# A language-model tower on one core: attention's side work dealt out anew over the heads' turns

## The chip, the core and the metric

One core of one Trainium2 chip. The metric is the device time of one execution in microseconds, the median of several; the profile is one more execution, recorded by the hardware profiler. Engines: TensorE (PE), VectorE (DVE), ScalarE (ACT), GpSimd (POOL), and SyncE (SP), which issues DMAs.

## What is computed

2048 tokens of width 256 pass through an embedding, four linear-attention blocks, a small mixture of experts, then 16-head softmax attention over sequences of 256 tokens, and a large mixture of experts with 64 experts, 8 chosen per token and 256 places per expert. The change lies in the last two, which the kernel interleaves. Cut to that:

```python
def attn(x, Wq, Wp, bp):                       # x: layernorm of h, (8, 256, 256)
    xh = x.reshape(B, N, 16, 16)
    q = jnp.einsum('bnhd,hed->bnhe', xh, Wq)
    scores = jnp.einsum('bnhe,bmhe->bhnm', q, q) / NORM
    attn = jax.nn.softmax(scores, axis=-1)
    y = jnp.einsum('bhnm,bmhe->bnhe', attn, q).reshape(B, N, D)
    return y @ Wp.T + bp
...
    logits = x_flat @ gate_weight.T            # x_flat: layernorm of the new h
    scores = jax.nn.sigmoid(logits)
    sfc = scores + e_bias[None, :]
    group_scores = jax.lax.top_k(sfc.reshape(T, NG, E // NG), 2)[0].sum(-1)
    _, gidx = jax.lax.top_k(group_scores, TG)  # 4 of 8 groups, then 8 experts of them
...
    xe = jnp.zeros((E, CAP, H)).at[sorted_e, pos].set(tok_sorted, mode='drop')
    h = silu(einsum(xe, w1)) * einsum(xe, w3)
    ye = jnp.einsum('ecf,ehf->ech', h, w2)     # weighted and summed back per token
    shared = silu(x @ shared_gate.T) * (x @ shared_up.T) @ shared_down.T
```

## The kernel before

Attention and routing are one phase, `attention_router_phase`. Each engine has its own program, written out by hand; they meet at semaphores alone, so the order within an engine is fixed when the kernel is built. The outer loop of all of them runs over SEQS = 8 sequences `i` and HEADS = 16 heads `hd`; its counter `u = 16 * i + hd` goes from 0 to 127. Here one round of it is called a turn.

In a turn TensorE issues the head's scores shifted by their row maxima (`shifted`, L2278, into `a_pB`), ScalarE takes the exponential (L2551, into the ring `a_ET`), and TensorE computes scores of a later head for the maxima (`maxima`, L2254, into `a_pA`, two banks), which VectorE reduces (`maximum`, L2585, `nmax`). `maxima_by` says how far ahead: one and a half heads per turn until `AHEAD` turns beyond one whole sequence. When a sequence's 16 maxima are there, VectorE splits them into three bf16 parts (`split`, L2594 to L2600), TensorE transposes them in the turn of `turned_at` (`maxima_transposed`, L2264), ScalarE copies them to `nT`, and SyncE moves them into row places of `right`; the first `shifted` of that sequence waits for this DMA. Four heads at a time TensorE multiplies the exponentials with the values (`values`, L2294, `a_pO`), ScalarE copies (L2502), TensorE transposes (L2304), VectorE divides (`divide`, L2607, L2611). A finished sequence is transposed (L2315), copied (L2506), projected with `wp` (`project`, L2322) and added to `h` by VectorE (`add`, L2619), with its row statistics (L2622).

Two sequences are a chunk of CH = 512 tokens (four tiles of 128); there are NC = 4, numbered 0 to 3. A chunk's routing is SPAN = 32 steps `o`, and `routing_at(step)` tells every engine which steps its turn holds: chunk 0 from turn 44 and chunk 1 from turn 76, a step per turn; chunk 2 from turn 108, two per turn; chunk 3 behind the loop. Step 0 aggregates the statistics on VectorE (`measured`, L2653, L2655, `m_veps`; for chunk 0 after some 15 constants, L2627 to L2645). POOL makes scale and shift of the rows (`rows_measured`, L2193 to L2197, here the row scale), steps 4 to 7 write the normalised rows on ScalarE (L2512), 8 to 11 transpose and copy them (L2335, L2518), 12 is the logits (L2344), 13 the sigmoid, 14 to 24 find the chosen experts on VectorE (mask `m_Mb`, L2710), 25 is their ranks on TensorE (L2354 to L2357), 27 to 29 turn ranks into slots (`m_idx`, L2731), 30 counts the taken ones on TensorE (L2362), 31 tells how many scatters a tile needs (`ksteps`, L2742).

POOL's queue, in this order: for each chunk `l` first `rows_measured(l + 1)` (for l below 2), then two scatters of each of its four tiles once the slots are there (L2202, one indirect DMA per tile and choice), then each tile's further scatters, 0 to 6, in pairs under a condition on `ksteps`. `rows_measured(3)` stands between chunk 2's first and further scatters. After chunk 2's and after chunk 3's, `scatters_over` waits until all scatters issued so far have landed. Behind it POOL adds the experts' results to the output with indirect DMAs (L1699). SyncE loads the first experts' rows (L2160) once it is told that chunks 0 to 2 have landed.

## Time and profile before

| what | us |
|---|---|
| median of 3 runs | 1204.93 |
| lowest and highest | 1203.73, 1207.11 |
| the profiled execution | 1203.64 |
| its span, first to last instruction | 1202.0 |
| attention and routing loop within it | about 821.5 to 1005.3 |
| the last expert stretch, to the end | 1067.7 to 1202.0 |

In the whole span TensorE is busy 89%, VectorE 63%, ScalarE 48%, POOL 25%; these are means over stages with quite different limits. The eight sequences start, by their first `shifted` matmul, at 821.5, 843.6, 860.2, 880.0, 903.2, 929.5, 951.9 and 975.2 us. In a row of the windows view, after the stretch, stand its length in us, the busy time with the number of records of TensorE's matmuls, its weight loads, VectorE, ScalarE and POOL, then TensorE's mean granted clock, the DMA engines' share and GB/s. An fp32 matmul stands in the trace as two records. In a row of the page's groups, behind the bar, stand busy us, mean ns of one, and idle time before them. In a timeline row the numbers are start and duration in us, then engine, line, operation, what it writes and reads, its shape, the count, and in brackets the engine's idle time before it with what ended it.

### The profile page before, as it was taken

The numbers are of one execution on the slowest core, as the hardware profiler recorded it, in microseconds if no ns is written. First come the engines' busy times: TensorE is split into PE (matmuls) and PEld (weight loads), VectorE is DVE, ScalarE is ACT, GpSimd is POOL, SyncE is SP. The second block draws the span as 40 slices with busy tenths as digits, with TensorE's granted clock in tenths as the row PEclk, the third lists the DMA queues.
The fourth block names the chain that finished last, engine by engine and source line by source line (L and its number), as shares of the span: only waits on it lengthen the run. The fifth ranks groups of instructions, "written<-read, shape, count | busy, mean of one in ns | idle before, by whom it ended". The sixth has DMA issues, their size and how long they took to land. (4 is left out here: it accounts for less than half of the span.)

```text
span 1202.0 us, 16309 instructions
## 1 busy us (share of the span) xinstructions
PE 1073.6 (89%) x4812; PEld 706.6 (59%) x4812; DVE 754.4 (63%) x1971; ACT 574.1 (48%) x970; POOL 299.9 (25%) x302
## 2 busy tenths in 40 slices
PE   5899999999999999999999999887987787898861
PEld 4556567657656756765765666663554454576741
DVE  3677766775785776677577684656769755643320
ACT  2572563563464365356446443564664663033430
POOL 6040010010011001001020101224001767366753
PEclk9999999999999999999999999897988978899995
DMA  4300120220120221021270000087633310869775
GB/s 125 129 1 1 49 75 23 84 96 1 48 75 30 80 91 49 0 75 70 70 265 1 12 7 1 4 175 146 108 55 61 123 64 27 296 142 236 123 216 99
DMA packets 58644, 100.07 MB, mean 83 GB/s; under 512 B 12504, under 2 KB 39814, under 8 KB 58315
## 3 DMA queue, kind: packets, MB, share of 16 engines
q1 hardware_dynamic: 40379, 59.22, 18.6%
q0 software_dynamic: 18192, 40.01, 12.2%
q8 instruction: 30, 0.49, 0.2%
q14 instruction: 43, 0.35, 0.1%
HBM read 58.51 MB, written 51.82 MB: 92 GB/s over the span
## 5 line engine op out<-in xcount | busy, mean ns | idle before, releaser
L561 PE MATMUL b_ring<-left 128*128 128x256 f32 x960 | 212.1, 379 | 0.0
L551 PE MATMUL b_ring<-right,left 128*128 128x512 f32 x480 | 208.4, 592 | 0.0
L561 PEld LDWEIGHTS b_ring<-left 128*128 128x128 f32 x960 | 181.6, 190 | 24.8 <-issue 1.0
L1105 POOL TENSOR_TENSOR b_rstd<-b_veps,b_mhalf 128x4 f32<-128x4 f32 x31 | 36.7, 1185 | 560.2 <-DVE b_veps L1179 560.2
L551 PE MATMUL b_ring<-XT,b_wqkv 128*128 128x512 f32 x384 | 170.1, 592 | 0.0
L551 PEld LDWEIGHTS b_ring<-right,left 128*128 128x128 f32 x480 | 91.2, 190 | 114.8 <-issue 103.0
L851 ACT ACTIVATE left<-b_ring,b_cur 128x512 f32<-128x512 f32 x128 | 88.0, 687 | 62.5 <-PE b_ring L551 44.3
L551 PEld LDWEIGHTS b_ring<-XT,b_wqkv 128*128 128x128 f32 x384 | 71.8, 190 | 77.3 <-issue 76.5
L1291 DVE RECIPROCAL b_mixing<-b_mixing 128x1024 f32<-128x1024 f32 x16 | 104.8, 6553 | 0.5
L2551 ACT ACTIVATE a_ET<-a_pB 128x512 f32<-128x512 f32 x128 | 74.1, 595 | 42.9 <-PE a_pB L2278 42.0
L2585 DVE TENSOR_REDUCE nmax<-a_pA 128x2 f32<-128x512 f32 x112 | 74.2, 688 | 32.0 <-PE a_pA L2254 30.6
L2202 POOL DMA_INDIRECT xe<-m_row,m_idx x84 | 82.5, 982 | 41.6 <-issue 26.3
L901 ACT ACTIVATE b_mixing<-b_ring,b_ncur 128x512 f32<-128x512 f32 x64 | 44.0, 688 | 101.4 <-PE b_ring L551 101.3
L848 ACT ACTIVATE b_ffo<-b_ffo 128x512 f32<-128x512 f32 x32 | 20.1, 629 | 120.1 <-DVE b_ffo L1225 120.1
L1258 DVE TENSOR_TENSOR right<-b_ffo,right 128x1024 f32<-128x1024 f32 x16 | 19.6, 1224 | 76.1 <-ACT b_ffo L848 76.1
L2278 PE MATMUL a_pB<-right,left 99*128 99x256 bf16 x256 | 54.7, 301 | 8.9 <-ACTq L2483 4.9
L561 PE MATMUL b_ring<-b_wo,right 128*128 128x256 f32 x256 | 59.7, 388 | 2.9 <-DVE right L1295 2.9
L2254 PE MATMUL a_pA<-right,left 96*128 96x256 bf16 x224 | 47.8, 301 | 14.1 <-DVE nmax L2585 13.3
L561 PEld LDWEIGHTS b_ring<-b_wo,right 128*128 128x128 f32 x256 | 49.8, 195 | 10.3 <-DVE right L1295 3.3
L1225 DVE TENSOR_TENSOR b_ffo<-b_ring,b_rows 128x512 f32<-128x512 f32 x32 | 22.1, 690 | 51.7 <-PE b_ring L561 32.3
L1185 DVE SCALAR_TENSOR_TENSOR right<-right,b_mv,b_rows 128x256 f32<-128x256 f32 x128 | 53.3, 477 | 0.0
L1214 DVE BATCH_NORM_STATS2 b_stats<-right 128x6 f32<-128x256 f32 x128 | 45.0, 413 | 1.3
(410 smaller groups left out, 1773.2 us busy)
## 6 DMA issues: line engine op xcount, KB each, us to landing
xe<-b_nil POOLq DMA_DIRECT2D x16, 1284.0 KB, 6.0
left<-in_w SPq DMA_DIRECT2D x8, 1024.0 KB, 5.4
a_ET<-xe SPq DMA_DIRECT2D x18, 321.0 KB, 4.0
parts<-in_wexp SPq DMA_DIRECT2D x12, 384.0 KB, 4.3
b_wqkv<-in_wqkv SPq DMA_DIRECT2D x4, 768.0 KB, 4.6
b_rows<-in_rows SPq DMA_DIRECT2D x8, 384.0 KB, 5.5
right<-qparts SPq DMA_DIRECT2D x16, 192.0 KB, 4.9
left<-qparts SPq DMA_DIRECT2D x16, 192.0 KB, 5.3
```

Of the source, the lines that this page charges most:

```text
L551: last = pe.matmul(bank[:, :], lhsT(k), rhs(k), start=(k == 0), stop=(k == n_k - 1))
L561: last = pe.matmul(bank[:, j * D:(j + 1) * D], src[:, k, tile], weights[:, k, :], start=(k == 0), stop=(k == n_k - 1))
L851: act.activation(H[:, f, :], bank[:, :], ACT.Gelu_apprx_tanh, bias=col("b1", f)).then_inc(s_h, 1)
L901: act.activation(nqk[:, j, m, :], bank[:, :], ACT.Relu, scale=-1.0, bias=ncur[:, KD * j + m:KD * j + m + 1])
L1185: last = dve.scalar_tensor_tensor(src[:, j, :], src[:, j, :], mv[:, j, 0:1], gain, ALU.subtract, ALU.mult)
L1214: last = dve.bn_stats(stats[:, j, :], src[:, j, :])
L1291: chain.link(dve.reciprocal(rec, den))
L2202: pool.indirect_dma_start(g["xe"][0:SLOTS, :], bass.IndirectOffsetOnAxis(ap=idx[:, t, k:k + 1].bitcast(U32), axis=0), row[:, t, :], None, ...
L2254: last = pe.matmul(pA[hd % 2][:, nt, :], left[0:ROWS, slot, hd, nt * P:(nt + 1) * P], right[0:ROWS, slot, hd, :], start=True, stop=True)
L2278: last = pe.matmul(pB[hd % 2][:, mt, :], left[0:ROWS + SPLIT, slot, hd, mt * P:(mt + 1) * P], right[0:ROWS + SPLIT, slot, hd, :], start=Tr ...
L2551: act.activation(ET[:, hd % ERING, :, :], pB[hd % 2][:, :, :], ACT.Exp, scale=4.0).then_inc(s_e, 1)
L2585: dve.tensor_reduce(nmax[:, :, hd], pA[hd % 2][:, :, :], AX.X, ALU.max, negate=True).then_inc(s_m, 1)
```

## The change

- `AHEAD` is 16, not 8: the maxima run up to 32 heads ahead, at one and a half per turn up to turn 31. `turned_at` lets the transposition of the maxima follow two turns after they are ready, or in the third turn of the sequence before.
- SPAN is 35. The routing steps are grouped otherwise (three of VectorE's larger ones cut in two), and a table TURNS holds the turn of each step of each chunk. Ranks are step 27, slots step 32, the count of the taken 33, `ksteps` 34.
- VectorE's constants are made one or two a turn from turn 32 on, and the waits for them stand at step 14.
- `values` and `project` are issued in two halves in neighbouring turns; `add` moves by a turn, and the row statistics (`summed`) follow a turn later.
- On POOL, `rows_measured(3)` stands ahead of the last tile's further scatters of chunk 1.
- Waits of the transpositions are fitted to the new order. Behind the loop, steps 14 to 27 and 28 to 34 stand where 14 to 26 and 27 to 31 stood.

```diff
@@ -1495,9 +1495,19 @@
 LATE = 2 * (NEXP - EARLY)
 GROUPS = -(-(EARLY + LATE) // RINGX)
 
-SPAN = 32
+SPAN = 35
 ROUTED = NC - 1
 LISTED = SEQS * HEADS - 4
+
+
+TURNS = (
+    (47, 47, 47, 47, 49, 49, 50, 50, 51, 52, 53, 54, 55, 56, 57, 57, 58, 58,
...
+)
...
         ident, h, qn, xT, ones_b, before = (g[n] for n in ("ident", "h", "qn", "XT", "ones_b", "before"))
         NTS = SEQ // P
-        AHEAD, QRING = 8, 2
+        AHEAD, QRING = 16, 2
...
@@ -2090,21 +2100,13 @@
         def turned_at(n):
 
             ready = next(u for u in range(SEQS * HEADS) if maxima_by(u) >= HEADS * (n + 1))
-            return max(HEADS * (n - 1) + 3 * QUAD, ready + 2)
+            return max(HEADS * (n - 1) + 2, ready + 2)
 
         turns = {turned_at(n): n for n in range(1, SEQS)}
 
         def routing_at(step):
 
-            found = []
-            for l in range(ROUTED):
-                begun = HEADS * (2 * l + 2) + 12
-                pace = 1 if l + 1 < ROUTED else 2
-                for part in range(pace):
-                    o = pace * (step - begun) + part
-                    if 0 <= o < SPAN:
-                        found.append((l, o))
-            return found
+            return [(l, o) for l in range(ROUTED) for o in range(SPAN) if TURNS[l][o] == step]
 
...
@@ -2230,8 +2232,8 @@
                 for j in range(TPC):
                     scattered(l * TPC + j, True)
                 for j in range(TPC):
-                    if l + 1 == ROUTED and j == 0:
-                        rows_measured(l + 1)
+                    if l + 2 == ROUTED and j == TPC - 1:
+                        rows_measured(l + 2)
                     scattered(l * TPC + j, False)
                 if l + 1 >= ROUTED:
                     scatters_over(l + 1 - ROUTED)
                 pe.wait_ge(s_nr, 3 * n)
                 if n > 1:
                     pe.wait_ge(s_nte, n - 1)
-                    pe.wait_ge(s_h, n - 1)
+                if n > 2:
+                    pe.wait_ge(s_h, n - 2)
                 for nt in range(NTS):
                     last = pe.transpose(pM[:, nt * P:(nt + 1) * P], npart[:, nt, :], g["ident_b"][:, :])
                 last.then_inc(s_nt, 1)
...
-            def values(i, k):
+            def values(i, k, mt):
 
                 n, slot = QUADS * i + k, i % QRING
-                if k == 0:
-                    pe.wait_ge(s_qs, i + 1)
-                    if i < QRING:
-                        pe.wait_ge(s_q1, 2 * (i + 1))
-                pe.wait_ge(s_ot, n + 2)
-                pe.wait_ge(s_e, QUAD * (n + 1) + 2)
-                for mt in range(NTS):
-                    for part in range(QUAD):
-                        hd = k * QUAD + part
-                        last = pe.matmul(pO[part * HW:(part + 1) * HW, k % 2, :], qs[:, slot, mt, hd, :],
-                                         ET[:, hd % ERING, mt, :], start=(mt == 0), stop=(mt == NTS - 1))
-                last.then_inc(s_o, 1)
+                if mt == 0:
+                    if k == 0:
+                        pe.wait_ge(s_qs, i + 1)
+                        if i < QRING:
+                            pe.wait_ge(s_q1, 2 * (i + 1))
+                    pe.wait_ge(s_ot, n + 2)
+                    pe.wait_ge(s_e, QUAD * (n + 1) + 2)
+                for part in range(QUAD):
+                    hd = k * QUAD + part
+                    last = pe.matmul(pO[part * HW:(part + 1) * HW, k % 2, :], qs[:, slot, mt, hd, :],
+                                     ET[:, hd % ERING, mt, :], start=(mt == 0), stop=(mt == NTS - 1))
+                if mt == NTS - 1:
+                    last.then_inc(s_o, 1)
...
-                if i + 1 < SEQS:
-                    pe.wait_ge(s_nte, i + 1)
+                pe.wait_ge(s_nte, min(i + 2, SEQS - 1))
...
-            def project(i):
-                pe.wait_ge(s_yte, i + 1)
-                for nt in range(NTS):
-                    for k in range(KD):
-                        last = pe.matmul(pH[:, nt, :], yT[:, k, nt * P:(nt + 1) * P], wp[:, k, :], start=(k == 0), stop=(k == KD - 1))
-                last.then_inc(s_p, 1)
+            def project(i, nt):
+                if nt == 0:
+                    pe.wait_ge(s_yte, i + 1)
+                for k in range(KD):
+                    last = pe.matmul(pH[:, nt, :], yT[:, k, nt * P:(nt + 1) * P], wp[:, k, :], start=(k == 0), stop=(k == KD - 1))
+                if nt == NTS - 1:
+                    last.then_inc(s_p, 1)
...
-                if o == 25:
+                if o == 27:
                     ranks(l)
-                if o == 30:
+                if o == 33:
                     taken_counted(l)
...
-                    if hd in (7, 11, 15):
-                        values(i, hd // QUAD - 1)
-                    if i and hd == 3:
-                        values(i - 1, QUADS - 1)
+                    if hd >= 6 and hd % QUAD >= 2:
+                        values(i, hd // QUAD - 1, hd % 2)
+                    if i and hd in (2, 3):
+                        values(i - 1, QUADS - 1, hd % 2)
                     if hd in (9, 13):
                         quad_transposed(i, hd // QUAD - 2)
                     if i and hd in (1, 5):
                         quad_transposed(i - 1, hd // QUAD + 2)
                     if i and hd == 8:
                         y_transposed(i - 1)
-                    if i and hd == 10:
-                        project(i - 1)
+                    if i and hd in (10, 11):
+                        project(i - 1, hd % 2)
...
+            def summed(i):
                 dve.wait_ge(s_h, i + 1)
                 for t in range(NTS * i, NTS * (i + 1)):
                     last = dve.bn_stats(g["stats"][:, t, :], h[:, t, :])
                 last.then_inc(s_st, 1)
...
+            def constants(o):
+                if o == 0:
+                    dve.wait_ge(s_c, 9)
+                    dve.tensor_copy(first[:, :], first_i[:, :]).then_inc(s_cc, 1)
+                if o == 1:
+                    dve.tensor_copy(row[:, :, D], tok_i[:, :]).then_inc(s_cc, 1)
+                if o == 2:
...
+                if o == 16:
+                    dve.wait_ge(s_cc, 14)
+                    dve.tensor_scalar(expert[:, 1, :], expert[:, 1, :], float(-SPE * NEXP), None, ALU.add).then_inc(s_cc, 1)
...
-                    if l == 0:
-                        constants()
                     measured(l)
                 if o == 14:
                     dve.wait_ge(s_sc, l + 1)
+                    if l == 0:
+                        dve.wait_ge(s_cc, 15)
+                        dve.wait_ge(s_gw, 32)
                     link(dve.tensor_tensor(sfc[:, :, :], score[:, :, :], ebias[:, :].unsqueeze(1).to_broadcast([P, TPC, NEXP]), ALU.add))
...
                     link(dve.tensor_tensor(sums[:, :, 0:2], quarters[:, :, 0:2], quarters[:, :, 6:8], ALU.add))
+                    link(dve.tensor_reduce(gs[:, :, :].rearrange("p t g -> p (t g)"), sums[:, :, :], AX.X, ALU.max))
                 if o == 19:
-                    link(dve.tensor_reduce(gs[:, :, :].rearrange("p t g -> p (t g)"), sums[:, :, :], AX.X, ALU.max))
-
                     other = gs[:, :, :].unsqueeze(2).to_broadcast([P, TPC, NG, NG])
                     own = gs[:, :, :].unsqueeze(3).to_broadcast([P, TPC, NG, NG])
                     dve.tensor_tensor(gt[:, :, :].rearrange(sq4, g=NG), other, own, ALU.is_gt)
...
-                if o == 27:
+                if o == 29:
                     dve.wait_ge(s_rk, l + 1)
                     dve.tensor_tensor(slot[:, :, :], ranked, first[:, :].unsqueeze(1).to_broadcast([P, TPC, NEXP]), ALU.add)
                     link(dve.scalar_tensor_tensor(valid[:, :, :], ranked, float(CAP), M[:, :, :], ALU.is_lt, ALU.mult))
...
-                if o == 29:
+                if o == 31:
                     dve.memset(g["carrier"][:, :], 0.0)
                     for j in range(TPC):
                         last = dve.max(s8[:, j, :], slot1[:, j, :])
                     link(last)
+                if o == 32:
                     dve.tensor_scalar(idx[:, l * TPC:(l + 1) * TPC, :], s8[:, :, :], -1.0, None, ALU.add).then_inc(s_ix, 1)
                     dve.tensor_scalar(v8b[:, :], s8[:, :, :].rearrange("p t k -> p (t k)"), 0.5, None, ALU.is_gt).then_inc(s_v8, 1)
...
-                    if i and hd == 11:
+                    if i and hd == 12:
                         add(i - 1)
+                    if i and hd == 13:
+                        summed(i - 1)
+                    constants(u - 2 * HEADS)
                     for l, o in routing_at(u):
                         routed(l, o)
```

Where the instructions stand now. TensorE, sequence 1's first turns: `a_pB` is a turn's shifted scores, `a_pA` the maxima's scores, two matmuls a head. Before:

```order
L2278 MATMUL a_pB<-right,left 128x256 x2
L2254 MATMUL a_pA<-right,left 128x256 x2
L2278 MATMUL a_pB<-right,left 128x256 x2
L2254 MATMUL a_pA<-right,left 128x256 x2
L2304 MATMUL a_pR<-ident,a_OT 128x128 x2
L2278 MATMUL a_pB<-right,left 128x256 x2
L2254 MATMUL a_pA<-right,left 128x256 x2
L2278 MATMUL a_pB<-right,left 128x256 x2
L2254 MATMUL a_pA<-right,left 128x256 x2
L2294 MATMUL a_pO<-a_ET,a_qs 32x256 x8
```

and now:

```order
L2281 MATMUL a_pB<-right,left 128x256 x2
L2256 MATMUL a_pA<-right,left 128x256 x4
L2281 MATMUL a_pB<-right,left 128x256 x2
L2256 MATMUL a_pA<-right,left 128x256 x2
L2308 MATMUL a_pR<-ident,a_OT 128x128 x2
L2281 MATMUL a_pB<-right,left 128x256 x2
L2256 MATMUL a_pA<-right,left 128x256 x4
L2297 MATMUL a_pO<-a_ET,a_qs 32x256 x4
L2281 MATMUL a_pB<-right,left 128x256 x2
L2256 MATMUL a_pA<-right,left 128x256 x2
L2297 MATMUL a_pO<-a_ET,a_qs 32x256 x4
```

Every second turn has the scores of two heads, and the values come in two groups of four.

VectorE, from chunk 0's maxima over slots (`m_s`) to the start of its step counts (`m_kcnt`). Before (turns 73 to 75):

```order
L2729 MAX m_s<-m_kept 128x8 x4
L2731 TENSOR_SCALAR m_idx<-m_s 128x32
L2732 TENSOR_SCALAR m_v8b<-m_s 128x32
L2585 TENSOR_REDUCE nmax<-a_pA 128x2
L2734 TENSOR_TENSOR m_cum<-m_cum,m_mch 128x64
L2735 CAST taken<-m_cum 128x128
L2585 TENSOR_REDUCE nmax<-a_pA 128x2
L2619 TENSOR_TENSOR h<-h,a_pC 128x512
L2622 BN_STATS stats<-h 128x6 x2
L2738 TENSOR_SCALAR m_some<-m_pG 1x32
L2739 TENSOR_REDUCE m_kcnt<-m_some 1x4
L2740 TENSOR_SCALAR m_kcnt<-m_kcnt 1x4
```

and now (end of turn 79 to turn 82):

```order
L2671 BN_AGGR m_mv<-stats 128x2 x4
L2673 TENSOR_SCALAR m_veps<-m_mv 128x4
L2591 TENSOR_REDUCE nmax<-a_pA 128x2
L2747 MEMSET carrier 128x1
L2749 MAX m_s<-m_kept 128x8 x4
L2591 TENSOR_REDUCE nmax<-a_pA 128x2
L2752 TENSOR_SCALAR m_idx<-m_s 128x32
L2753 TENSOR_SCALAR m_v8b<-m_s 128x32
L2755 TENSOR_TENSOR m_cum<-m_cum,m_mch 128x64
L2756 CAST taken<-m_cum 128x128
L2591 TENSOR_REDUCE nmax<-a_pA 128x2
L2759 TENSOR_SCALAR m_some<-m_pG 1x32
```

The slots now follow chunk 1's statistics (`m_veps`); before they preceded them.

POOL, from chunk 1's last tile to chunk 2's first scatters (each pair of scatters stands under a condition). Before:

```order
L2215 COMPARE_AND_BRANCH
L2202 DMA xe<-m_row,m_idx 16384x321 x2
L2215 UNCONDITIONAL_BRANCH
L2202 DMA xe<-m_row,m_idx 16384x321 x8
L2193 TENSOR_TENSOR m_rstd<-m_veps,m_mhalf 128x4
L2195 TENSOR_TENSOR m_shift<-m_mv,m_rstd 128x4
L2197 TENSOR_SCALAR m_shift<-m_shift 128x4
```

and now:

```order
L2204 DMA xe<-m_row,m_idx 16384x321 x2
L2217 UNCONDITIONAL_BRANCH
L2195 TENSOR_TENSOR m_rstd<-m_veps,m_mhalf 128x4
L2197 TENSOR_TENSOR m_shift<-m_mv,m_rstd 128x4
L2199 TENSOR_SCALAR m_shift<-m_shift 128x4
L2215 TENSOR_LOAD ksteps
L2215 ISA x2
L2217 COMPARE_AND_BRANCH
L2204 DMA xe<-m_row,m_idx 16384x321 x2
L2217 UNCONDITIONAL_BRANCH
L2217 COMPARE_AND_BRANCH
...
L2204 DMA xe<-m_row,m_idx 16384x321 x2
L2217 UNCONDITIONAL_BRANCH
L2204 DMA xe<-m_row,m_idx 16384x321 x8
```

The row scale (`m_rstd`, `m_shift`) has moved ahead of the tile's scatters and of the eight.

## Rows read from the trace of the kernel before

**Rows 1.** Windows: sequences 1 to 6, chunk 2's chain, the stretch behind attention.
```profile
843.64:860.21 16.57, 16.02 (x150) 9.69 (x151) 13.04 (x27) 11.24 (x24) 0.00 (x0) 1.00 0.46 78
860.21:880.04 19.83, 17.05 (x150) 9.89 (x151) 15.54 (x49) 11.17 (x24) 1.46 (x3) 0.91 0.64 114
880.04:903.22 23.18, 20.22 (x179) 13.72 (x175) 14.73 (x34) 17.18 (x33) 0.00 (x0) 0.93 0.26 46
903.22:929.49 26.27, 19.21 (x170) 10.65 (x166) 24.75 (x84) 11.90 (x24) 1.97 (x4) 0.90 0.33 58
929.49:951.88 22.39, 19.51 (x178) 13.11 (x175) 14.69 (x34) 16.99 (x33) 17.21 (x18) 0.96 0.35 126
951.88:972.59 20.71, 15.22 (x135) 8.92 (x131) 19.63 (x73) 10.23 (x22) 11.80 (x13) 0.92 0.16 57
972.59:1005.30 32.71, 24.43 (x177) 14.98 (x176) 16.91 (x74) 18.06 (x34) 24.76 (x27) 0.74 0.19 64
1005.30:1067.67 62.37, 52.75 (x216) 34.81 (x217) 32.52 (x119) 13.41 (x25) 31.18 (x34) 0.92 0.55 179
```

**Rows 2.** Waits, 821 to 1006 us: waiter, releaser, total us, times, longest.
```profile
PEld a_pA L2254 <- DVE nmax L2585: 26.0, 44, 2.8
...
PE m_pG L2354 <- DVE m_Mb L2710: 6.0, 3, 2.8
...
PE a_pB L2278 <- DMA right<-nT: 3.2, 3, 2.1
```

**Rows 3.** VectorE, a run of maxima (timeline); the matmuls for the maxima (page).
```profile
844.29 2.49 DVE L2585 TENSOR_REDUCE nmax<-a_pA 128x2 f32<-128x512 f32 x4 [2.37 <-PE a_pA L2254]
...
L2254 PE MATMUL a_pA<-right,left 96*128 96x256 bf16 x224 | 47.8, 301 | 14.1 <-DVE nmax L2585 13.3
```

**Rows 4.** Windows: the constants, a split, two comparisons, slots with counts, step counts.
```profile
874.36:876.40 2.04, 0.61 (x4) 0.31 (x4) 1.90 (x16) 1.23 (x3) 0.00 (x0) 1.00 0.04 12
917.63:918.39 0.76, 0.74 (x6) 0.53 (x6) 0.66 (x4) 0.76 (x2) 0.00 (x0) 1.00 0.00 0
1027.75:1028.54 0.79, 0.79 (x6) 0.69 (x5) 0.76 (x2) 0.00 (x0) 0.00 (x0) 1.00 1.02 386
1040.25:1041.57 1.32, 1.32 (x6) 1.02 (x5) 1.22 (x9) 0.00 (x0) 0.00 (x0) 0.54 0.98 377
1044.69:1045.64 0.95, 0.95 (x3) 0.38 (x3) 0.84 (x5) 0.00 (x0) 0.70 (x1) 1.00 1.02 387
```

**Rows 5.** Timeline, POOL: scatters of the four chunks, row scales, the first expert sum.
```profile
928.99 1.13 POOL L2202 DMA_INDIRECT xe<-m_row,m_idx  x1 [0.61 <-issue]
...
966.37 0.97 POOL L2202 DMA_INDIRECT xe<-m_row,m_idx  x1 [0.30 <-issue]
972.85 1.04 POOL L2193 TENSOR_TENSOR m_rstd<-m_veps,m_mhalf 128x4 f32<-128x4 f32 x1 [5.51 <-DVE m_veps L2655]
...
1016.88 1.08 POOL L2202 DMA_INDIRECT xe<-m_row,m_idx  x1 [1.11 <-issue]
...
1041.87 0.97 POOL L2202 DMA_INDIRECT xe<-m_row,m_idx  x1 [14.96 <-DVE m_idx L2731]
...
1067.67 1.58 POOL L1699 DMA_INDIRECT sums<-a_qs,x_home  x1 [5.68 <-ACT a_qs L1799]
```

**Rows 6.** Timeline, VectorE: chunk 0's slots and chunk 2's statistics.
```profile
921.49 0.18 DVE L2731 TENSOR_SCALAR m_idx<-m_s 128x32 int32<-128x32 f32 x1
...
972.59 0.17 DVE L2655 TENSOR_SCALAR m_veps<-m_mv 128x4 f32<-128x4 f32 x1
```

**Rows 7.** Timeline, SyncE's queue; then DMA issues: KB and us to landing.
```profile
1042.34 4.52 SPq L2160 DMA_DIRECT2D a_ET<-xe  x3
...
sums<-a_qs,x_home POOLq DMA_INDIRECT x2, 4.3
```

**Rows 8.** Timeline, TensorE: the logits of chunk 0 and of chunk 2.
```profile
891.61 1.97 PE L2344 MATMUL m_pG<-m_gate,XT 128*128 128x64 f32 x16
...
980.39 3.67 PE L2344 MATMUL m_pG<-m_gate,XT 128*128 128x64 f32 x16 [0.26 <-ACT XT L2518]
```

81 lines of the change are left out of this document (43 added, 38 removed), and 5 rows, old and new, of the table TURNS.

## The prediction

> **What bounds the kernel now.** I read the busy time by stretches first [rows 1]. The change touches 843 us to 1005 us, the attention over eight sequences of 16 heads; I call the step in which TensorE issues one head's shifted scores a turn (0 to 127), and a stretch of [rows 1] is 16 turns, up to the last two. Sequence 1 takes 16.57 us with TensorE busy 16.02: TensorE sets it. Sequence 4 takes 26.27 us with VectorE busy 24.75 (0.94): VectorE sets it, because it has the maxima of 16 heads and most of a chunk's routing. Sequence 6 has VectorE busy 19.63 of 20.71. In sequences 3 and 5 nobody is full; TensorE waits in turns for VectorE and ScalarE. The waits of TensorE say the same [rows 2]: weight loads waited 26.0 us for a maximum (two PSUM banks, so TensorE is at most two heads ahead of VectorE), matmuls 6.0 us for the routing mask and 3.2 us for the row of shifts. From 972.59 to 1005.30 one chain sets the time: chunk 2's statistics, POOL's row scale, ScalarE's rows, the logits, then some 30 small VectorE operations. Behind attention, TensorE is busy 52.75 of 62.37 us, and this stretch's order is nearly unchanged. So the end moves by what the last chain's start moves, if POOL, which scatters rows, keeps up [rows 5].
>
> **Part 1: maxima 16 heads ahead.** Turns 16 to 31 now carry 24 maxima, not 16, and turns 96 to 103 carry none. One costs VectorE 0.60 us (four in 2.49 us, where the last one's end still overlaps the next, [rows 3]); TensorE pays at most 0.43 (47.8 us busy for 224 matmuls, two a head, and back to back they overlap). Sequence 1's VectorE sum becomes 13.04 + 8 x 0.60 + 0.8 (one more split of maxima into parts, [rows 4]) = 18.6 us, beside TensorE's 16.02 and at most 3.4 more. At sequence 4's ratio of 0.94 it takes 19.8 us: **+3.2** (bounds +2, if both overlap fully, and +5). In exchange the shift rows (turn 18, 34, ... instead of 28, 44, ...) have landed at each later sequence's start; only sequence 1's first wait, 2.1 of the 3.2 us [rows 2], stays. In sequence 6 VectorE loses nine maxima and a split, 6.2 us: 19.63 - 6.2 = 13.4, and I add 3 us in which VectorE and TensorE wait for each other (mask, ranks, projection): 16.4 against 20.71, **-4.3** (bounds -2 and -6).
>
> **Part 2: constants one by one.** Before, VectorE makes all constants in turn 44, 2.04 us from 874.36 on, just after a sum and before the statistics [rows 4]. They hold up maxima, TensorE waits, and its clock is at half afterwards (0.91 and 0.93 granted in sequences 2 and 3, [rows 1]). Now each turn has one of 0.1 to 0.3 us. Sequence 2's VectorE sum stays 15.54 us; over 0.94 that is 16.5, and I take 16.8 against 19.83: **-3.0** (bounds -1.5 and -3.5).
>
> **Part 3: the chunk steps.** Chunk 0's 35 steps run over turns 47 to 82 (before 32 over 44 to 75). In sequence 3 nothing is left in turns 60 to 63, and the start is at full clock: I take **-2.4** of 23.18 (bounds 0 and -3.5; TensorE is busy 20.22 of it, part of that at half clock). In sequence 4, the two group comparisons come in (0.79 us), and the last maxima over slots, the sums of counts and the step counts go out into turns 80 to 82: in chunk 3's rows these are 1.32 and 0.95 us [rows 4]. Net -1.5: 24.75 becomes 23.3, over 0.94 24.8: **-1.4** (bounds 0 and -2.5). Sequence 5 gets these 2.3 us, but had VectorE busy 14.69 of 22.39, and its last four turns lose steps too: 0 (bounds -1 and +2). Values and projection cut in halves cost TensorE nothing, since the matmuls are the same; a block of 1.1 us becomes two. I give them nothing of their own.
>
> Up to turn 80 that makes +3.2 - 3.0 - 2.4 - 1.4 = **-3.6 us**, up to chunk 2's statistics -7.9.
>
> **Part 4: what POOL then does.** This is the step that I expect to decide. Chunk 0's slots are now ready in turn 81, not in turn 73 (921.49 us, [rows 6]). Before, chunk 1's row scale stood ahead of its scatters in POOL's queue, and they began at 928.99 [rows 5]. Now: turn 80 at 929.49 - 3.6 = 925.9, plus two maxima (1.2), the maxima over slots (0.64) and the slots (0.17): 927.9, first scatter at 928.3. The 30 scatters last 38.35 us (928.99 to 966.37, + 0.97), and behind them in POOL's queue stands chunk 2's row scale: 966.7, while VectorE has its input ready at 972.76 - 7.9 = 964.9 [rows 6]. Before it was the other way round: POOL had idled 5.51 us when it began at 972.85. So of 7.9 us, 972.85 - 966.7 = 6.1 arrive. The chain behind it has the same operations; ScalarE's rows now have one more head's exponential between them: +0.6. I take **-5.5 us** for the end of attention.
>
> **Part 5: chunk 3's row scale ahead of chunk 1's last tile.** POOL now stops there until attention is over, and then has that tile's later scatters (2 to 6) and chunk 2's 16 still to issue, 18 to 22 times 1.28 us = 23 to 28 us. On the old time base: from 1016.9 to 1040 - 1045, where chunk 3's slots are ready at 1041. Before, POOL idled 14.96 us there [rows 5]; that idle time is the cover, and it is used up. What is late next is POOL's wait for the landing of these scatters, which it needs before chunk 3's. No row shows a landing of this line; the nearest is POOL's indirect sum at 4.3 us [rows 7], and zero is the other end. So chunk 3's scatters start 0 to 8 us late, and the first expert sum at 1067.67 can absorb up to 5.7 us between the last scatter's end and it [rows 5]: cost 0 to 2.5, I take 0, as the tile with the fewest kept rows should have 2. SP loads the first experts' rows at 1042.34 [rows 7], 25 us ahead of the first sum; 8 us late they still land 12 us ahead of it, and cost nothing.
> For the landing, the Trainium skill (DMA: Bandwidth & Descriptors, Anatomy of one DMA — SWDGE (gpsimd) path) has a fit of 2.0 us and the bytes over 436 GB/s; an estimate by it for 164 KB is 2.4 us, and the cost would be 0 to 1. No run here shows it.
>
> **Sum.** The profiled execution took 1203.64 us (span 1202.0 and 1.6 around it), 1.3 below the median of 1204.93. 1203.6 - 5.5 = 1198.1; on the median **1199.4 us**.
>
> **The rivals.**
> A. *Side work decides, not POOL* (0.12): the first scatter is early enough, or the later sequences gain more. Then most of 7.9 and more arrives: 1195 to 1196. For it: sequences 3 and 5 have slack on every engine. Against: 38.35 us of scatters is a hard length.
> B. *The gain shrinks* (0.22): sequence 1 costs 5, or sequence 3 gives nothing, so turn 80 moves by only 1 us; then the first scatter is at 930.9 and the row scale at 969.3, gain 3; or Part 5 costs 2.5. 1201 to 1203.5.
> C. *It does not do what it says* (0.08): VectorE's sum over turns 16 to 127 is unchanged, and if TensorE's waits only move, from sequence 6 into 1, the time is 1204 to 1206. Against: sequence 1 has 3.5 us of idle VectorE, sequence 7's chain has no maxima to move.
> D. *Slower through the scatters* (0.10): chunk 0's scatters begin eight turns later. From a first scatter at 934.5 on, POOL reaches the row scale after 972.85 and everything is late by the rest. That needs turn 80 at 932.2, 2.7 us later than before, so sequence 1 at +5, sequences 3 and 4 at 0, and sequence 5's added steps in full: 1206, and up to 1211 where the chain behind is longer too.
> E. *Slower through TensorE's clock* (0.06). The logits took 1.97 us at the high level (2.4 GHz) and 3.67 us in sequence 7, where the granted clock of the stretch was 0.74 after TensorE had waited for rows [rows 8, 1]. Without maxima in turns 96 to 103 and with more waiting for POOL, TensorE is less busy there; if sequence 6's projection, values and transposes also ran at 1.2 GHz it would cost 2 to 4 us, and the gain is 2: 1203, or with B 1206.
> The Trainium skill (TensorE: Matmul & The Clock Gate, Part 1: The HAM clock gate) says that the throttled state is the default and that activity releases it. By it E is the likelier, the more work leaves TensorE; the sum above has the clock as before.
>
> **How the numbers follow.** Forecast, 1197 to 1201.3: 0.42. A 0.12, B 0.22, C 0.08, D 0.10, E 0.06. About 0.3%, 3.6 us, is what a measurement can tell from no change, so faster is below 1201.3: forecast and A in full, a quarter of B: 0.60. Slower is above 1208.5: D's upper half and E with it, 0.09. The rest, 0.31, is within. The range takes A in and goes up to D's lower part: 1194.5 to 1206.5.
>
> **What would show it.** In the changed profile: sequence 1 near 19.8 us with VectorE above 0.9; no TensorE wait for shift rows but the first; sequence 2 near 17; POOL's first scatter near 928, chunk 2's row scale right behind chunk 0's last scatter without idle, near 967; POOL idle some 12 us before chunk 3's row scale near 1008.5, and little before chunk 3's scatters; the first expert sum near 1062. I am wrong if sequence 1 takes over 22 us, if POOL idles before chunk 2's row scale (then A), if the first scatter is after 931 (B, D), or if the stretch from row scale to attention's end is over 34 us (E).

## The result: slower by 0.9%

The changed kernel took 1214.40 us as the median of four executions (1212.46 to 1216.67), the kernel before 1204.66 in the same comparison; the ratio is 1.009, with a 95% interval of 1.0062 to 1.0117. In a second comparison, called f1_again below, it was 1.0105 (1.0073 to 1.0137). The prediction was 1199.4 with a range up to 1206.5: wrong in sign, and out of range.

The profiled execution took 1212.46 us, its span is 1210.8, and its mean granted clock is 0.954, as before. Windows of the changed kernel, with the columns of [rows 1]: sequences 1 to 6 (6 up to chunk 2's statistics), chunk 2's chain, the stretch behind attention.

```profile
845.28:868.59 23.31, 20.34 (x167) 11.38 (x167) 17.47 (x34) 11.89 (x23) 0.00 (x0) 0.93 0.35 62
868.59:885.70 17.11, 16.36 (x155) 9.41 (x151) 14.09 (x40) 11.75 (x24) 0.00 (x0) 1.00 0.54 96
885.70:912.93 27.23, 21.24 (x179) 12.87 (x175) 16.16 (x45) 17.52 (x33) 1.46 (x3) 0.94 0.35 60
912.93:935.15 22.22, 19.17 (x168) 9.82 (x165) 21.02 (x61) 12.26 (x24) 0.00 (x0) 0.92 0.42 73
935.15:963.34 28.19, 22.07 (x179) 13.18 (x176) 17.97 (x58) 17.82 (x33) 18.72 (x21) 0.88 0.28 98
963.34:984.28 20.94, 15.80 (x129) 7.96 (x125) 15.00 (x67) 11.35 (x23) 12.41 (x13) 0.84 0.29 98
984.28:1016.80 32.52, 21.69 (x172) 11.21 (x170) 16.89 (x74) 17.89 (x32) 21.39 (x23) 0.84 0.11 35
1016.80:1080.41 63.61, 54.36 (x226) 36.65 (x227) 33.23 (x123) 13.77 (x26) 34.87 (x37) 0.92 0.56 183
```

Against [rows 1], sequence 1 is 6.7 us longer, 3 by 4.1 and 5 by 5.8; sequence 2 is 2.7 shorter and 4 by 4.1. Sequence 6 up to chunk 2's statistics and the chain behind it are as long as before, to 0.2 us. From sequence 0's first shifted scores to the end of the add of sequence 7 it is 11.7 us more: 8.0 of them in sequences 1 to 6, 3.0 from sequence 7's start on and 0.7 in sequence 0. The waits of the same stretch, 822 to 1017 us, in the columns of [rows 2]:

```profile
PEld a_pA L2256 <- DVE nmax L2591: 19.1, 37, 1.4
...
PE m_pG L2358 <- DVE m_Mb L2729: 5.5, 2, 2.8
...
PE a_pC L2325 <- ACT a_yT L2512: 4.9, 2, 2.4
...
PE a_pB L2281 <- ACT a_ET L2557: 3.9, 3, 1.9
...
PE m_pG L2366 <- DVE m_v8b L2753: 3.6, 2, 2.8
...
PE a_pB L2281 <- DMA right<-nT: 1.5, 1, 1.5
```

The two waits that the change was read for are shorter: weight loads for a maximum 26.0 to 19.1, shift rows 3.2 in three to 1.5 in one. Three others have come or grown: the projection's for ScalarE's copy of y, twice 2.4 us (before 0.7 at most), the shifted scores' for an exponential, all in sequence 7, and the count's of the taken for the slots. POOL's timeline, the rows that answer to [rows 5]:

```profile
940.90 1.13 POOL L2204 DMA_INDIRECT xe<-m_row,m_idx  x1 [1.13 <-DVE m_idx L2752]
...
984.45 1.04 POOL L2195 TENSOR_TENSOR m_rstd<-m_veps,m_mhalf 128x4 f32<-128x4 f32 x1 [5.04 <-DVE m_veps L2673]
...
1026.77 1.04 POOL L2195 TENSOR_TENSOR m_rstd<-m_veps,m_mhalf 128x4 f32<-128x4 f32 x1 [14.46 <-DVE m_veps L2673]
...
1057.20 0.97 POOL L2204 DMA_INDIRECT xe<-m_row,m_idx  x1 [4.65 <-DMA xe<-m_row,m_idx]
...
1080.41 1.58 POOL L1709 DMA_INDIRECT sums<-a_qs,x_home  x1 [3.08 <-DMA xe<-m_row,m_idx]
```

POOL idles 5.04 us ahead of chunk 2's row scale, as it did before. The scatters, which I expected to decide, decide nothing here.

### The profile page after: what moved, and what is told of

Same layout as the page of the kernel before. It is cut to its first block and busy times, and to the rows that moved or that the text cites. A ratio compares the mean times of both kernels' runs of the same rounds, so it can differ in the third digit from the quotient of the medians.

```text
span 1210.8 us, 16301 instructions
## 1 busy us (share of the span) xinstructions
PE 1080.4 (89%) x4812; PEld 702.2 (58%) x4812; DVE 752.9 (62%) x1971; ACT 577.8 (48%) x970; POOL 301.0 (25%) x302
## 3 DMA queue, kind: packets, MB, share of 16 engines
q1 hardware_dynamic: 40379, 59.22, 18.6%
## 5 line engine op out<-in xcount | busy, mean ns | idle before, releaser
L561 PEld LDWEIGHTS b_ring<-left 128*128 128x128 f32 x960 | 181.8, 190 | 24.6 <-issue 1.0
L848 ACT ACTIVATE b_ffo<-b_ffo 128x512 f32<-128x512 f32 x32 | 20.1, 629 | 120.1 <-DVE b_ffo L1225 120.1
L1225 DVE TENSOR_TENSOR b_ffo<-b_ring,b_rows 128x512 f32<-128x512 f32 x32 | 22.1, 691 | 51.6 <-PE b_ring L561 32.2
L2297 PE MATMUL a_pO<-a_ET,a_qs 128*32 128x256 f32 x512 | 46.6, 442 | 0.5 <-ACT a_OT L2508 0.5
```

Of the source, the lines that this page charges most:

```text
L561: last = pe.matmul(bank[:, j * D:(j + 1) * D], src[:, k, tile], weights[:, k, :], start=(k == 0), stop=(k == n_k - 1))
L2297: last = pe.matmul(pO[part * HW:(part + 1) * HW, k % 2, :], qs[:, slot, mt, hd, :], ET[:, hd % ERING, mt, :], start=(mt == 0), stop=(mt == ...
```

## Where sequences 3 and 5 went, read from the trace

ScalarE's timeline of turns 56 to 58 in the changed kernel:

```profile
899.98 0.60 ACT L2557 ACTIVATE a_ET<-a_pB 128x512 f32<-128x512 f32 x1 [1.74 <-PE a_pB L2281]
900.59 1.28 ACT L2528 ACT_TABLE_LOAD   x1
901.89 0.38 ACT L2528 ACTIVATE m_score<-m_pG 128x256 f32<-128x256 f32 x1
902.29 1.28 ACT L2557 ACT_TABLE_LOAD   x1
903.58 0.60 ACT L2557 ACTIVATE a_ET<-a_pB 128x512 f32<-128x512 f32 x1
904.08 0.59 ACT L2512 ACTIVATE a_yT<-a_pC 128x512 f32<-128x512 f32 x1
```

and of TensorE at that time:

```profile
900.00 0.60 PE L2318 MATMUL a_pC<-ident,a_y 128*128 128x128 f32 x4
...
901.63 0.64 PE L2297 MATMUL a_pO<-a_ET,a_qs 128*32 128x256 f32 x8
904.72 0.77 PE L2325 MATMUL a_pC<-wp,a_yT 128*128 128x256 f32 x1 [2.45 <-ACT a_yT L2512]
```

The same turns of the kernel before, on ScalarE:

```profile
893.84 0.60 ACT L2551 ACTIVATE a_ET<-a_pB 128x512 f32<-128x512 f32 x1 [1.88 <-PE a_pB L2278]
894.33 0.59 ACT L2506 ACTIVATE a_yT<-a_pC 128x512 f32<-128x512 f32 x1
894.94 1.28 ACT L2522 ACT_TABLE_LOAD   x1
896.24 0.38 ACT L2522 ACTIVATE m_score<-m_pG 128x256 f32<-128x256 f32 x1
896.64 1.28 ACT L2551 ACT_TABLE_LOAD   x1
```

The sigmoid needs a table of its own and the exponential behind it the old one: 1.28 + 0.38 + 1.28 us, 3.0 with the gaps. Before, step 13 stood in turn 57 behind the copy of y. Now it is in turn 56, ahead of it, and the projection of turn 58 waits for all of it. Chunk 1 has the same in turn 90. The Trainium skill (ScalarE: Activation LUTs, What ACT_TABLE_LOAD costs) gives 1283 ns for the load, as here, and 1380 ns for a drain beside it. The trace shows no such drain: 1.31 us lie between the exponential's end and the sigmoid.

VectorE in turns 80 and 81 of the changed kernel:

```profile
937.89 0.17 DVE L2673 TENSOR_SCALAR m_veps<-m_mv 128x4 f32<-128x4 f32 x1
937.97 0.68 DVE L2591 TENSOR_REDUCE nmax<-a_pA 128x2 f32<-128x512 f32 x1
...
938.71 0.46 DVE L2749 MAX8 m_s<-m_kept 128x8 f32<-128x64 f32 x3
939.21 0.69 DVE L2591 TENSOR_REDUCE nmax<-a_pA 128x2 f32<-128x512 f32 x1
939.82 0.17 DVE L2752 TENSOR_SCALAR m_idx<-m_s 128x32 int32<-128x32 f32 x1
939.90 0.18 DVE L2753 TENSOR_SCALAR m_v8b<-m_s 128x32 bf16<-128x32 f32 x1
```

Steps 32 and 33 of chunk 0 share turn 81. TensorE issues the count (33) in that turn and waits 2.79 us for the slots (32), since VectorE is behind by chunk 1's statistics, the maxima over slots and two maxima of scores. Its clock is at half from 938.91 to 945.74, and turn 82 has 2.17 us.

## The experiments

The experiments ask four things in turn: what each part of the change costs by itself, what comes back when a part is taken out of the changed kernel, what the halved blocks do, and whether the good parts alone make a faster kernel.

A word on the measuring. The kernel before was executed 132 times beside the experiments, 1196.12 to 1213.39 us. These times go with the mean granted clock: 0.63 us less for each 0.001 more (correlation -0.76; 0.959 in the fastest, 0.947 in the slowest). One trace is one such draw: the attention's first scores began anywhere from 818.6 to 827.8 us, in front of everything that was changed, and the last expert stretch, behind it, took 130.4 to 134.8 us. So totals are told by the ratios over many executions, and a trace only tells where something happened. The table gives, from one trace each, the time from one sequence's first shifted scores to the next one's, and from sequence 0's first to the end of the add of sequence 7.

| kernel | parts | ratio, 95% interval | seq 1 | 2 | 3 | 4 | 5 | 6 | 0 to add 7 |
|---|---|---|---|---|---|---|---|---|---|
| before | | 1 | 16.6 | 19.8 | 23.2 | 26.3 | 22.4 | 23.3 | 191.1 |
| changed | all | 1.0090, 1.0062-1.0117 | 23.3 | 17.1 | 27.2 | 22.2 | 28.2 | 21.6 | 202.8 |
| f1_again | all | 1.0105, 1.0073-1.0137 | 23.6 | 17.1 | 27.2 | 22.2 | 31.1 | 20.7 | 205.9 |
| e1_ahead | A | 1.0012, 0.9983-1.0042 | 22.2 | 20.4 | 23.4 | 26.6 | 22.7 | 19.4 | 194.6 |
| e2_constants | C | 0.9965, 0.9940-0.9989 | 16.6 | 17.1 | 22.2 | 26.1 | 22.2 | 24.4 | 190.5 |
| e3_halves | H | 1.0017, 0.9988-1.0046 | 17.2 | 19.1 | 22.8 | 26.2 | 21.6 | 24.6 | 192.4 |
| e4_turns | T | 1.0025, 0.9997-1.0053 | 16.6 | 16.6 | 26.1 | 23.0 | 25.2 | 28.5 | 193.4 |
| f2_no_ahead | C H S T P | 1.0093, 1.0060-1.0126 | 18.2 | 18.6 | 28.6 | 22.7 | 25.8 | 27.3 | 202.7 |
| f3_score_back | A C H S T' P | 1.0033, 1.0009-1.0056 | 22.1 | 17.1 | 25.2 | 21.9 | 25.7 | 21.5 | 195.9 |
| f4_late_ahead | C, A late | 0.9956, 0.9935-0.9978 | 16.6 | 17.1 | 22.2 | 25.4 | 25.7 | 19.8 | 189.0 |
| g1_const_turns | C T' | 0.9985, 0.9968-1.0003 | 17.9 | 16.8 | 22.7 | 22.2 | 23.1 | 28.8 | 189.9 |
| g2_spread_late | C T'', A late | 0.9965, 0.9938-0.9993 | 16.6 | 16.8 | 21.7 | 22.2 | 29.2 | 18.9 | 184.4 |
| g3_pool_as_before | A C H S T' | 1.0042, 1.0024-1.0061 | 23.6 | 17.1 | 24.0 | 22.2 | 24.6 | 21.4 | 194.5 |
| g4_no_ahead_13 | C H S T' P | 1.0055, 1.0023-1.0087 | 18.2 | 18.5 | 22.7 | 22.8 | 23.8 | 27.2 | 195.7 |
| h1_whole_values | A C T' | 0.9988, 0.9963-1.0013 | 23.4 | 17.2 | 24.8 | 22.0 | 24.1 | 20.6 | 194.6 |
| h2_halves_kept | A C H T' | 1.0083, 1.0046-1.0119 | 23.5 | 17.5 | 23.7 | 23.4 | 24.7 | 18.5 | 199.0 |
| h3_combined | C T''', A late | 0.9946, 0.9918-0.9974 | 16.6 | 16.8 | 21.7 | 23.3 | 26.2 | 21.4 | 189.2 |
| i1_changed_whole | A C S T P | 1.0042, 1.0029-1.0055 | 23.0 | 17.2 | 25.7 | 21.8 | 29.5 | 20.1 | 194.6 |
| i2_values_halved | A C T', values halved | 1.0021, 0.9992-1.0050 | 23.6 | 17.5 | 23.6 | 22.2 | 25.5 | 20.9 | 192.6 |
| i3_project_halved | A C T', project halved | 1.0042, 1.0023-1.0061 | 24.0 | 17.8 | 24.2 | 23.2 | 24.9 | 18.5 | 199.4 |

A is the maxima ahead with their transposition, C the constants dealt out, H values and projection in halves, S add in a sequence's turn 12 and statistics in 13, T the regrouped steps with TURNS, P POOL's order. T', T'' and T''' are tables mended as told below.

### Each part alone

Each is the kernel before with hunks of the change. A, which also has the two waits of the transpositions fitted:

```diff
-        AHEAD, QRING = 8, 2
+        AHEAD, QRING = 16, 2
-            return max(HEADS * (n - 1) + 3 * QUAD, ready + 2)
+            return max(HEADS * (n - 1) + 2, ready + 2)
```

> The kernel before with part 1 of the change alone: AHEAD 16, turned_at two turns after the maxima are ready or in turn 2 of the sequence before, and the two waits of the transpositions fitted to it. Theory L (each part cost what its own sequence shows): sequence 1 grows by about 6 us over before's 16.57, to 22 to 23; no wait for shift rows after the first; sequence 6 falls by 2 to 4 from 23.32; sequence 4 falls from 26.27 a little; end of attention +1 to +4 against 1005.3. Theory I (sequence 1 grew in the changed kernel because the extra maxima meet the values in halves): with whole values sequence 1 is 18.5 to 20.5, as I had forecast (19.8), and the end of attention comes 0 to 3 us earlier.

Sequence 1 took 22.19 us, with whole values: the first theory. Only the first wait for shift rows is left, and sequence 6 fell by 3.9. Its window in this kernel, and in f3_score_back, where the clock is at full in it:

```profile
850.08:872.27 22.19, 19.36 (x166) 11.69 (x166) 17.83 (x35) 11.68 (x23) 0.00 (x0) 0.92 0.32 55
```
```profile
841.42:863.47 22.05, 18.94 (x166) 10.66 (x167) 17.31 (x34) 11.90 (x23) 0.00 (x0) 1.00 0.42 72
```

With VectorE busy 17.3 and TensorE 18.9 of 22.05, neither is full, and the clock is not the reason. VectorE's idle time has not shrunk: 16.57 - 13.04 = 3.5 us before [rows 1], 22.05 - 17.31 = 4.7 now. Most of it lies where TensorE runs values and the projection (beside the projection gaps of 1.8 us before, and of 1.3 and 1.4 us in f3_score_back). Two banks of scores are all that VectorE has to work on meanwhile; that this is why more maxima don't fill it is my reading of the order, and no run with more banks was made. They come on top: 4.3 us of VectorE's work made 5.5 us of time.

The constants alone (C; `constants(u - 2 * HEADS)` in each turn, the waits at step 14):

> The kernel before with VectorE's constants alone dealt out over turns 32 to 48, and their waits at step 14. Both theories: sequence 2 falls from 19.83 to about 17, as in the changed kernel (17.11), everything else as before, the end of attention 2 to 3 us earlier, total about 1202. Rival: the block of constants was harmless, sequence 2 fell in the changed kernel because its maxima had run ahead; then sequence 2 stays at 19 to 20 and the total is unchanged.

Sequence 2 fell to 17.14 us, and the ratio's interval (0.9940 to 0.9989) lies below 1: this part is a small gain of its own. In the one trace the 3.8 us that it led at sequence 5 shrank to 0.5 by the add of sequence 7.

H alone, with the add in turn 11 as before:

```diff
+                    if hd >= 6 and hd % QUAD >= 2:
+                        values(i, hd // QUAD - 1, hd % 2)
...
+                    if i and hd in (10, 11):
+                        project(i - 1, hd % 2)
```

> The kernel before with values and project in two halves in neighbouring turns alone (add and row statistics where they were). Theory H (two small blocks cost TensorE more than one, since each half starts anew and waits for the exponentials one turn earlier): every sequence from 1 on grows by 0.5 to 1.0 us, end of attention +3.5 to +7. Theory N (they cost nothing of their own, as I had forecast): every sequence within 0.3, end within 1 us, unless they fill a turn in which TensorE waits anyway.

Neither theory: sequences 1 and 6 are longer, 2 and 5 shorter, and the ratio's interval holds 1.

T alone (TURNS and SPAN = 35; the constants in one block, now in turn 47):

> The kernel before with the routing steps regrouped to 35 and the table TURNS alone (constants still in one block, now in turn 47). Theory S (the sigmoid, now one turn ahead of ScalarE's y copy, makes the projection wait; slots and counts of chunk 0 now in one turn behind chunk 1's statistics): waits of TensorE of about 2.4 us each in turns 58 and 90 for ScalarE's y copy and 2 to 3 us in turn 81 for VectorE; sequences 3 and 5 come to about 26 to 28 us (before 23.18 and 22.39), the first scatter near 940, the end of attention +5 to +9. Theory L (packing cost only together with the other parts): sequences 3 and 5 within 1.5 of before, end within 2.

Waits of TensorE from sequence 0 to 1000 us:

```profile
PE a_pC L2324 <- ACT a_yT L2508: 6.8, 3, 3.0
...
PE m_pG L2364 <- DVE m_v8b L2736: 3.5, 2, 2.4
```

The projection waited 3.0 us in turns 58 and 90; turn 81's wait was 1.1, and 2.4 came in turn 104, where chunk 1's slots and count are neighbours. Sequences 3 and 5 grew by 3.0 and 2.8 (26.1 us as expected, and 25.2, a little under it) and 6 by 5.2, but 2 and 4 shrank by 3.2 and 3.3, and 2.1 us went behind sequence 7's start, so the sum was +2.3 and not +5 to +9.

The four ratios add up to +0.2%, not +0.9%. S and P are in none of them. Either the changed kernel's executions were late by chance, or parts hurt each other, or S or P costs by itself.

> The changed kernel once more, beside the others of this comparison. The four single parts gave 1.0012, 0.9965, 1.0017 and 1.0025 of before, which add up to +0.2%, while the changed kernel had 1.009 in four executions. Theory of adding up by the trace: from sequence 0's first shifted scores to the add of sequence 7 the parts alone gave +3.5, -0.5, +1.3 and +2.3 us, and 2.7 of the constants' gain is in two of them, so +9.3 of the 11.7 us that the changed kernel took longer there: the ratio comes out again at 1.006 to 1.010, sequence 1 at 22 to 24, sequences 3 and 5 at 26 to 28. Rival, the first executions were late by chance: ratio 1.001 to 1.004.

It was 1.0105: not chance. P is taken out below (1.0042 against 1.0033, no difference); S was never run alone, so what is left is that parts hurt each other or that S does.

### Taking parts away from the changed kernel

Without A:

> The changed kernel without part 1: AHEAD 8, turned_at and the two waits as before. Adding up: sequence 1 at 17 to 17.5, sequence 6 at 24 to 26 in place of 21.6, sequence 0's start to sequence 7's add at 198 to 200 us (changed kernel 202.8, before 191.1), ratio 1.004 to 1.006. Rival, the maxima ahead hurt the packed steps: sequences 3 and 5 fall back below 24.5 as well and the ratio is 1.001 or less.

A miss: 1.0093, no better than with it. Sequence 1 fell to 18.2 us, but a wait had come:

```profile
PE a_pC L2266 <- DVE h L2625: 8.2, 6, 1.5
```

The old place of the maxima's transposition is turn 12, and it waits for the previous sequence's add, which S has moved to turn 12. The undoing had made a new wait, so it doesn't price A. With the transposition in turn 13, `max(HEADS * (n - 1) + 3 * QUAD + 1, ready + 2)`, and the table T':

> As the kernel with the sigmoid and the counts moved, and without the maxima ahead; unlike the first undoing, the transposition of the maxima stands in the sequence's turn 13, behind VectorE's add (turn 12), for which it waited 8.2 us in all. Adding up: sequence 1 at 17 to 18 in place of 22.05, sequence 6 two to four us above 21.5, waits of that transposition under 2 us in all, ratio 0.999 to 1.002. Rival, removing the lead costs as much in the later sequences as it gives in sequence 1: ratio 1.003 to 1.005.

1.0055 beside 1.0033 with A: outside the theory's range, a little above the rival's, and the two intervals overlap. Six such waits are left with 5.7 us, and shift rows are waited for seven times, 7.0 us. Sequence 1 gives 3.9 us back and sequence 6 takes 5.8. Where S is in, taking A out gains nothing.

The sigmoid behind the copy of y, and the counts apart from the slots (T'):

```diff
-    ... 54, 55, 56, 57, 57, 58, 58, 59, 64, ..., 76, 80, 81, 81, 82),
+    ... 54, 55, 57, 58, 58, 59, 59, 60, 64, ..., 76, 80, 81, 82, 83),
-    ... 86, 87, 88, 89, 89, 90, 91, 91, 96, ...
+    ... 86, 87, 89, 90, 90, 91, 91, 92, 96, ...
```

> The changed kernel with the sigmoid one turn later (57 and 89, behind ScalarE's y copy, with steps 14 to 18 a turn later), and chunk 0's counts in turns 82 and 83 in place of 81 and 82. Theory S: the projection's waits of 2.4 us in turns 58 and 90 fall to about 0.3, turn 81's wait of 2.8 us to under 0.8; sequences 3 and 5 lose 2 to 3 and 3 to 5 us, sequence 0's start to sequence 7's add comes to 195 to 198 us, ratio 1.002 to 1.005. Rival, these waits lie beside others and come back elsewhere in the same sequence: both sequences within 1 us of 27.2 and 28.2.

Median 1208.97 against 1216.67 in the same comparison, 7.7 us less, and intervals that don't meet. The projection's waits of 2.4 us are gone. Turns 58 and 59, as windows of the changed kernel and of this one:

```profile
901.10:909.38 8.28, 5.83 (x35) 3.16 (x33) 4.11 (x13) 5.00 (x8) 0.00 (x0) 0.79 0.01 2
897.13:901.63 4.50, 4.30 (x34) 2.35 (x32) 3.19 (x9) 4.44 (x7) 0.00 (x0) 1.00 0.00 0
```

The kernel before also has 4.50 us there. Turns 90 and 91 take 6.7 us in the changed kernel and 4.5 in the other two, turns 81 to 83 take 9.4 in the changed kernel and 7.9 in this one: together 3.8 + 2.2 + 1.5 = 7.5 us, about as much as the medians are apart. Sequence 3 as a whole is 2.1 us shorter than in the changed kernel and 5 by 2.5, less than those turns give: in this trace the clock was at half for 6.8 us early in either sequence (from 884.48 and 932.27 us). This is most of the loss, shown. One run moved the sigmoid and the counts together, so their shares are read from these turns alone; and the mean granted clock, 0.953 here and 0.946 in f1_again, may have come of the waits or added to the difference by chance. ScalarE now has:

```profile
897.38 0.59 ACT L2509 ACTIVATE a_yT<-a_pC 128x512 f32<-128x512 f32 x1
897.99 1.28 ACT L2525 ACT_TABLE_LOAD   x1
899.28 0.38 ACT L2525 ACTIVATE m_score<-m_pG 128x256 f32<-128x256 f32 x1
```

POOL's order as before, on top of that (`l + 1 == ROUTED and j == 0`):

> The changed kernel with the sigmoid behind the y copy and the counts apart (ratio 1.0033 before), and now also POOL's order as before: chunk 3's row scale behind chunk 2's first scatters. Theory P (with the scatters behind it, POOL waits 4.65 us for their landing ahead of chunk 3's scatters, and this ends in the first expert sum): the stretch from sequence 7's add to the first sum falls from 56.0 to 53.5 to 54.5 us, with no wait for a landing above 0.5 us behind TensorE's part. Rival (the wait for the landing is covered, as I had forecast): 55 to 56 us again.

```profile
1048.93 0.97 POOL L2201 DMA_INDIRECT xe<-m_row,m_idx  x1 [14.99 <-DVE m_idx L2749]
...
1074.70 1.58 POOL L1706 DMA_INDIRECT sums<-a_qs,x_home  x1 [5.63 <-ACT a_qs L1806]
```

The landing wait is gone, and chunk 3's first scatter starts 29.3 us behind the add of sequence 7, not 32.4. From that add to the first expert sum it takes 55.1 us, not 56.0: outside what the theory gave, inside the rival's 55 to 56, and nothing that the ratio shows. The change's cost here is covered.

### Whole blocks against halves

g1_const_turns has C and T' alone:

> The kernel before with two parts, the constants dealt out and the regrouped steps with their table, in which the sigmoid stands in turns 57 and 89, behind the y copy, and chunk 0's counts in turns 82 and 83. Theory S (what the table cost was the sigmoid's and the counts' place): against the table alone 2 x 2.3 us and some 1.5 us less, so 187 to 188 us from sequence 0's start to sequence 7's add (before 191.1, table alone 193.4), ratio 0.996 to 0.999. Rival, the packed steps are slow in themselves: 190 us and more, ratio 1.000 or above.

0.9985: the regrouped steps, mended, cost nothing that the ratio shows, though the trace's 189.9 us lie between the two theories. With A as well, and then with H:

> The kernel before with the maxima ahead from sequence 1 on, the constants dealt out and the mended table; values and projection whole, add and row statistics where they were, POOL as before. Theory V (the halves and the later add carry the rest of the loss, since without them and without the lead the ratio was 0.9985, and the lead alone was 1.0012): ratio 0.998 to 1.000, sequence 0's start to sequence 7's add 187 to 190 us. Rival W (the maxima ahead carry it, 5.5 us in sequence 1, won back only in part): ratio 1.002 to 1.004, 192 to 195 us.

> The same with values and projection in halves, add and row statistics still in the sequence's turn 11. If the halves carry the loss, as high as the version with the later add: ratio 1.003 to 1.004, each of the sequences 1 to 6 some 0.5 us longer than with whole values. If the later add carries it, 0.998 to 1.000. By the halves' own run (1.0017) I expect +0.1 to +0.2% against whole values.

0.9988 and 1.0083. V held by the ratio (the one trace, with 194.6 us and sequence 1 at 23.4, lies where W would have it), and the halves cost far more than their own run had let me expect. The order on VectorE and TensorE suggested the projection; each alone:

> The version with maxima ahead, constants dealt out and mended table (0.9988 with whole blocks, 1.0083 with both in halves), now with the values alone in halves. Theory: the values carry it, since there are 32 of them and 8 projections, and they sit in the turn in which the scores of two heads are due: 1.005 to 1.009. Rival, the projection carries it: 0.998 to 1.001.

> The same with the projection alone in halves; its second half is issued in turn 11, the turn in which VectorE adds it, so VectorE waits with later maxima behind the add. Theory (values carry it): 0.998 to 1.001. Rival (VectorE, waiting for the second half, delays the maxima queued behind its add): 1.004 to 1.008 and the values alone near 1.000.

1.0021 and 1.0042: the values fall short of the theory's range, the projection is where the rival has it. Both may have a share; against 0.9988 only the projection's is apart by its interval. TensorE and then VectorE in turns 122 and 123 of i3_project_halved:

```profile
1004.68 1.91 PE L2321 MATMUL a_pC<-wp,a_yT 128*128 128x256 f32 x4
1006.39 0.63 PE L2278 MATMUL a_pB<-right,left 99*128 99x256 bf16 x2
1006.95 1.94 PE L2294 MATMUL a_pO<-a_ET,a_qs 128*32 128x256 f32 x16
1008.81 1.21 PE L2321 MATMUL a_pC<-wp,a_yT 128*128 128x256 f32 x4
1012.00 0.19 PE L2362 MATMUL m_pG<-m_v8b,ones_b 128*128 128x32 bf16 x1 [1.98 <-DVE m_v8b L2746]
```
```profile
1006.88 0.46 DVE L2742 MAX8 m_s<-m_kept 128x8 f32<-128x64 f32 x3
1010.12 0.69 DVE L2620 TENSOR_TENSOR h<-h,a_pC 128x512 f32<-128x512 f32 x1 [2.78 <-issue]
1010.84 0.75 DVE L2623 BATCH_NORM_STATS2 stats<-h 128x6 f32<-128x256 f32 x2
1011.51 0.41 DVE L2745 TENSOR_SCALAR m_idx<-m_s 128x32 int32<-128x32 f32 x1
```

The second half of the projection stands behind the values of turn 123. VectorE's add waits 2.78 us; the row names no releaser, but the second half ends at 1010.02 and the add starts at 1010.12. Chunk 2's slots are queued behind the add, and TensorE then waits for the slots. Turns 122 and 123 take 7.8 us, with a whole projection (h1_whole_values) 5.9. That is 1.9 us of some 6 that lie between the ratios; in sequences 1 to 5 the same two turns are 0 to 0.2 us longer, and the mean granted clock over all executions was 0.948 against 0.953. A second place is the end: from turn 127 to the end of sequence 7's add, i3_project_halved takes 12.2 us at a granted clock of 0.68 and h2_halves_kept 12.4 at 0.50, h1_whole_values 9.8 at 0.85. Whether the wait in turn 123 had brought the clock down isn't shown. The rest has no place in the traces. In the changed kernel the add comes a turn later. There:

> The changed kernel with values and projection whole again, everything else as changed (ratio of the changed kernel 1.009 and 1.0105). Theory V (the halves carry 0.5 to 0.9% here too): ratio 1.001 to 1.005; with the sigmoid and the counts mended on top it would be that of before. Rival (they cost only with the add in turn 11, as in the run before): 1.008 to 1.010.

1.0042 instead of 1.0090 and 1.0105, as V has it, and the intervals don't meet. But the size is loose: the kernel before had a median of 1206.41 in this comparison, 1.7 to 3.6 us above the others, and between the medians of the changed kernel, 1214.40 and 1216.67, and this one's 1213.0 lie only 1.4 and 3.7 us. The traces have the same two places. Turns 122 and 123 take 6.0 and 6.2 us in the changed kernel's two traces and 4.3 here; from turn 126 to the end of the add it is 10.9 and 10.9 at a clock under 0.9, here 9.0 at full clock. With halves at full clock (g3_pool_as_before) it is 9.2, so the second place is the clock's. Beside h1_whole_values (0.9988) this kernel has S, P and the table that isn't mended: 0.5% more, no more than the table's places cost between f3_score_back and f1_again (0.7%). So S shows no cost of its own, and what is left is that parts hurt each other.

### Towards a better version

The same eight maxima, made in sequence 5 instead of 1, with C:

```diff
+            more = min(AHEAD, max(0, (step - 5 * HEADS + 2) // 2))
-            return min(SEQS * HEADS, HEADS + min(step + 1 + AHEAD, (3 * (step + 1) + 1) // 2))
+            return min(SEQS * HEADS, HEADS + min(step + 1 + AHEAD + more, (3 * (step + 1) + 1) // 2))
```

> The kernel before with the constants dealt out, and the eight maxima ahead not made in sequence 1 but in sequence 5, one and a half a turn over turns 80 to 95; transpositions and waits as before. Theory M (a maximum ahead costs 0.7 us in sequence 1, where TensorE and VectorE hand two banks to and fro without a gap, and little in sequence 5, where VectorE was busy 14.7 of 22.4 us): sequence 5 grows by 0 to 2 us, sequence 6 falls by 3.5 to 4.5 us against 24.4, the ratio is 0.992 to 0.996. Rival: a maximum ahead costs 0.7 us anywhere, sequence 5 grows by 5 to 6 us and the ratio is 0.996 to 1.000.

0.9956, better than before, though not shown to be better than C alone, whose interval (0.9940 to 0.9989) overlaps this one's. Sequence 5 grew by 3.5 us (C alone: 22.2), between the two theories: 0.43 us a maximum, not 0.69 as in sequence 1. Sequence 6 fell by 4.6. A table with more spread (T'': statistics in turns 45 and 77, group steps of chunk 1 in 92 to 95):

> The kernel before with the constants dealt out, the maxima ahead in sequence 5, and a table with steps spread further: chunk 0's statistics in turn 45 and chunk 1's in 77, rows a turn earlier, sigmoids in 57 and 89, chunk 1's group steps over turns 92 to 95 that were empty, counts apart from slots. Theory: 1 to 2 us better than the constants and the table without it, 184 to 187 us, ratio 0.993 to 0.997; TensorE's wait for the rows in turn 51 under 0.5 us. Rival: VectorE's idle time in turns 92 to 95 lies where TensorE runs blocks, so steps put there delay the maxima; sequence 5 grows by as much as sequence 6 falls, ratio 0.996 to 1.000.

Both came in part: 184.4 us and 0.9965, and sequence 5 at 29.2, 6 at 18.9. But not for the rival's reason: of the 3.5 us by which sequence 5 is longer than in f4_late_ahead, turns 92 to 95 have 0.9 (8.2 us against 7.3) and turns 80 to 88 have 2.5 (15.7 against 13.2), where this table packs the rows and transpositions of chunk 1. T''' has chunk 1 back at one step a turn, 76 to 107:

> The kernel before with the constants dealt out, chunk 0's steps by the spread table (statistics in turn 45, sigmoid in 57, counts in 82 and 83), chunk 1's at before's pace of one a turn (turns 76 to 107), chunk 2's packed, and the eight maxima ahead in sequence 5. If gains add up: sequences 2, 3 and 4 as in the spread version (16.8, 21.7, 22.2 us), 5 and 6 together 45.5 as in the version with the late lead alone, 184 to 187 us in all, ratio 0.991 to 0.995. Rival: what is gained up to sequence 4 is given back in 5 to 7, as in the versions before (constants alone 3.8 gained, 3.3 given back), where TensorE's clock and chunk 2's chain set the time: ratio 0.995 to 0.998.

0.9946, 1196.34 us: the lowest ratio of all, and faster than both kernels, though its interval (0.9918 to 0.9974) overlaps those of C alone and of the two before it. Its trace has 189.2 us for attention, not 184 to 187, so part of the gain is given back in sequences 5 to 7, as the rival has it.

## Why the prediction was wrong, by its own steps

- **What bounds the kernel.** The sum went by VectorE's and TensorE's busy time. In turns 56 to 58, and again in 88 to 90, the chain ran over ScalarE, which has slack in every row of [rows 1].
- **Part 1.** The mechanism was right, sizes were off. Sequence 1: +3.2 forecast, bounds +2 and +5; +6.7 in the changed kernel, +5.6 in e1_ahead. The failed term is "at sequence 4's ratio of 0.94": sequence 1 reached 0.79 (17.31 of 22.05). Sequence 6 took 20.94 us up to the statistics, not 16.4: the split and the last maximum still fell into it, so VectorE was busy 15.0 us and not 13.4, and waits took 5.9 us and not the 3 that I had added. To the start of sequence 7 it gained 1.7 us (3.9 in e1_ahead alone), but the statistics follow a later add.
- **Part 2** held: -2.7 for -3.0, and 0.9965 for C alone. "Sequence 2's VectorE sum stays 15.54 us" was off: it is 14.1, since chunk 0's statistics and one maximum now fall behind the sequence's end.
- **Part 3** is where the sign was lost. It priced the VectorE operations of each moved step and forgot that step 13 is a ScalarE step with two table loads, which the new turn puts ahead of the copy of y; TensorE's waits of 2.4 us in turns 58 and 90, and of 2.8 us in turn 81 for slots that share the count's turn, stand at nothing in the sum. Sequence 3 came at +4.1, not -2.4, and sequence 5 at +5.8, not 0. Mending these places gave 7.7 us back. It did not bring the forecast gain: the kernel stayed at 1.0033, and sequence 3 took 22.7 us (g1_const_turns) to 25.2 (f3_score_back), not 20.8. Sequence 4 gained 4.1, not 1.4. "Values and projection cut in halves cost TensorE nothing" was wrong as well: alone they cost 0.2%, with an interval that holds 1, beside the other parts 0.5 to 0.9%. What the sentence left out is who waits for the second half: 1.9 us in turns 122 and 123 of i3_project_halved, and some 2 us at a lower clock behind them; the rest has no place.
- **Part 4** never came to bear. Turn 80 came at 935.15 us, not 925.9, and the slots 4.7 us behind it, not 2.0. VectorE's input for chunk 2's row scale came 11.6 us later than before, and POOL idled.
- **Part 5** held. The tile had two further scatters, 18 were left, and their landing cost POOL 4.65 us, inside 0 to 8. By the fit in the Trainium skill (DMA: Bandwidth & Descriptors, Anatomy of one DMA — SWDGE (gpsimd) path) it would have been 2.4 us; the measurement decides. The 5.7 us of slack were used up, to the point that the first sum now waits for the landing of scatters (3.08 us) and not for ScalarE. Cost 0 to 1.
- **The rivals.** None held this. D had the first scatter after 934.5 and was right that it would be late (940.9), but its mechanism, POOL late at the row scale, did not occur. For E, sequence 6 had a clock of 0.84 in place of 0.92, but chunk 2's chain 0.84 in place of 0.74. The 0.09 for slower was far too little: there was no rival for a new wait on the one engine that no part of the sum had looked at.

The sum in the end, by ratios: A, C and T' 0.9988; with the halves and the later add 1.0042; with POOL's order 1.0033, the same; with the sigmoid and counts where the change puts them 1.0090 and 1.0105.

## What to carry to other kernels

When steps are packed or moved by a table, walk through every engine's queue at each new place and ask what stands behind the moved instruction, above all on the engine with slack: a sigmoid between exponentials is not 0.38 us but 3.0. Idle time of an engine counts as room only if its input can arrive in it; here eight more maxima did not fill VectorE's idle time beside TensorE's long blocks. And an undone part can leave a wait that the whole change had moved out of the way, so a part is priced by adding it and by taking it out.

## What the runs showed of the hardware

- The kernel before spread over 17 us in 132 executions, with 0.63 us for each 0.001 of mean granted clock; among the traces, the code in question starts up to 9.3 us apart.
- A switch of ScalarE's table costs 1.31 us from one activation's end to the next one's start, and two of them with a sigmoid 3.0.
- POOL waited 4.65 us (5.12 in f3_score_back) for the landing of its last scatters when 18 had been issued back to back.
